# Layer 1's preparation in twenty slices, big products dealt out singly between the stages, and layer 1's first input split during layer 0's last pair

## What is computed

```python
def _layer(x, style, w, b, mw, mb, typ):
    s = style @ mw.T + mb
    weight = SCALE * w * s[:, None, :, None]
    demod = lax.rsqrt(jnp.sum(weight * weight, axis=(2, 3)) + EPS)
    weight = weight * demod[:, :, None, None]
    ...                       # conv, transposed conv + blur, conv, blur + strided conv; + b
x = x + einsum('bsd,ed->bse', cond0(x, style), identity)                 # layer 0
y = cond1(x, style)                                                      # layer 1
base = einsum('bth,oh->bto', y, W_base) + b_base
z, logits = y @ A[active], (y @ router_W + router_b)[active]
alpha = softmax(log(prior[active] + eps) + logits)
x = x + base + einsum('bteo,bte->bto', (z @ B[active]) * 2, alpha)
```

## Time and profile before

| | us |
|---|---|
| median of three runs | 1620.59 |
| lowest and highest | 1616.82, 1621.03 |
| the profiled execution | 1616.13 |
| its span, first to last instruction | 1614.3 |
| PE busy in it | 1516.0 (94%) |
| DVE, ACT, POOL busy | 1045.2, 754.4, 466.3 |

### The profile page before, as it was taken

The page is one execution under the profiler, slowest core; times in us unless marked ns, Lnnn a source line. Parts: engine busy times, 40 slices in busy tenths (PEclk is TensorE's granted clock), DMA queues, the critical chain, the costliest instruction groups (busy, mean ns, idle before and its releaser), DMA issues.

```text
span 1614.3 us, 29276 instructions
## 1 busy us (share of the span) xinstructions
PE 1516.0 (94%) x9655; PEld 1394.1 (86%) x9655; DVE 1045.2 (65%) x2447; ACT 754.4 (47%) x1675; POOL 466.3 (29%) x537
## 2 busy tenths in 40 slices
PE   4888888899999999999988999999999999999998
PEld 4677777788888888888876999999999999999998
DVE  7745676555665565566566676677667766776674
ACT  3434353254544555554443454455445545554452
POOL 2213132132233333223321322332233223322330
PEclk9999998899999999999998999999999999999999
DMA  4251321233333333333233233233323332333221
GB/s 102 79 134 54 100 58 53 58 100 104 104 104 97 85 79 102 104 104 104 78 112 113 63 104 104 78 77 104 104 78 78 104 104 79 77 104 104 80 76 65
DMA packets 54336, 145.72 MB, mean 90 GB/s; under 512 B 17233, under 2 KB 19345, under 8 KB 54306
## 3 DMA queue, kind: packets, MB, share of 16 engines
q1 hardware_dynamic: 53616, 144.96, 33.1%
q10 hardware_dynamic: 690, 0.37, 0.1%
HBM read 111.75 MB, written 33.55 MB: 90 GB/s over the span
## 4 chain that ended last, share of the span: by engine, by line
PE 81%; DVE 13%; issue 3%; DMA 1%; POOL 1%; ACT 1%; DVEq 0%; SPq 0%; ACTq 0%; POOLq 0%
PE bank L1164 25%; PE bank L1166 24%; PE bank L1165 24%; PE bank L1438 4%; DVE conv_buf L1019 2%; DVE tw L1029 2%; DVE tw L1025 1%; PE bank L1311 1%; DVE conv_buf L1022 1%; PE bank L1375 1%; DMA xraw<-x_dram 1%; DVE w_l L848 0%; PE bank L1365 0%; DVE fw_l L929 0%; DVE conv_buf L1041 0%
## 5 line engine op out<-in xcount | busy, mean ns | idle before, releaser
L1164 PE MATMUL bank<-fw_h,ct_h 128*128 128x512 f32 (+2 forms) x1280 | 462.3, 361 | 0.5 <-DVE xout L901 0.5
L1166 PE MATMUL bank<-fw_h,ct_l 128*128 128x512 f32 (+2 forms) x1280 | 454.8, 355 | 0.0
L1165 PE MATMUL bank<-fw_l,ct_h 128*128 128x512 f32 (+2 forms) x1280 | 454.2, 355 | 0.0
L376 POOL COPY conv_buf<-edge 128x4 f32 (+1 forms) x128 | 20.5, 188 | 911.3 <-DVE tw L1029 910.9
L1166 PEld LDWEIGHTS bank<-fw_h,ct_l 128*128 128x128 f32 x1280 | 242.8, 190 | 23.5
L1164 PEld LDWEIGHTS bank<-fw_h,ct_h 128*128 128x128 f32 x1280 | 243.1, 190 | 17.9 <-issue 0.8
L1165 PEld LDWEIGHTS bank<-fw_l,ct_h 128*128 128x128 f32 x1280 | 243.5, 190 | 15.5
L536 ACT ACTIVATE z_h<-bank,lam_pairs 64x256 fp32r<-64x256 f32 (+1 forms) x256 | 113.4, 443 | 214.3 <-PE bank L1166 195.1
L1006 DVE TENSOR_SCALAR z_f<-bank,lam_pairs 64x256 f32<-64x256 f32 (+1 forms) x256 | 115.2, 450 | 146.8 <-PE bank L1166 139.1
L367 POOL TENSOR_TENSOR d_l<-d_f,d_h 128x512 fp32r<-128x512 f32 x128 | 158.0, 1235 | 133.0 <-ACT d_h L522 132.9
L362 POOL TENSOR_TENSOR d_f<-xraw 128x512 f32<-128x512 f32 x128 | 169.6, 1347 | 49.8 <-DMA xraw<-x_dram 29.5
(11 more groups left out here) (219 smaller groups left out, 3108.2 us busy)
## 6 DMA issues: line engine op xcount, KB each, us to landing
xraw<-in_x_dram SPq DMA_DIRECT2D x32, 512.0 KB, 6.6
xres<-in_x_dram SPq DMA_DIRECT2D x32, 512.0 KB, 4.2
x_dram<-xout SPq DMA_DIRECT2D x32, 512.0 KB, 2.9
xraw<-x_dram SPq DMA_DIRECT2D x32, 512.0 KB, 6.2
xres<-x_dram SPq DMA_DIRECT2D x32, 512.0 KB, 4.3
out_dram<-xout SPq DMA_DIRECT2D x32, 512.0 KB, 2.9
xraw<-in_x_dram SPq DMA_DIRECT2D x32, 511.5 KB, 8.0
xraw<-x_dram SPq DMA_DIRECT2D x32, 511.5 KB, 7.6
```

Of the source, the lines that this page charges most:

```text
L1164: mm(out, wh, xh, start=start, stop=False, skip_group_check=True)
L1165: mm(out, wh, xl, start=False, stop=False, skip_group_check=True)
L1166: return mm(out, wl, xh, start=False, stop=stop, skip_group_check=True)
```

## The change

1. `PREPS` goes from 7 to 20: the same preparation is cut into twenty slices for pairs 2 to 21, and the functions on DVE, ACT and PE are cut accordingly (`prep_kernels`, `prep_roots`, `prep_tables`, `prep_pack`, `prep_selected`, `prep_base`, `prep_m13`, `prep_w1`, `prep_m4`, `prep_first_turns`, `prep_rows(k0)`). Most PE parts now stand a body ahead of the slice that reads them, behind the last big product; only two quarters of `prep_rows` stand between convolutions. Pairs 22 to 30 are the loop of ACT and DVE.
2. The big products are placed by a running number: `ffn(ly, j, lo, hi)` issues the products lo to hi - 1, and a stage can stand inside a group of three. Their order among themselves is the old one. In layer 0: 8, 11, 14, 6, 9. In layer 1: 13, 17, 20, 10, 12.
3. Layer 1's first input is loaded, and split by POOL and ACT, at the end of layer 0's last pair. On POOL it stands ahead of the three low parts of layer 1's weights (line 400). The second input's load goes ahead of the last store of layer 0.

```diff
-PREP, PREPS = 2, 7
+PREP, PREPS = 2, 20
...
+                if not n:
+                    sp.wait_ge(s["x_ready"], 2 * NPAIR)
+                    sp.wait_ge(s["stored"], stores(2))
+                    load_x(second, 0)
+                    sp.wait_ge(zs["bb_ready"], 1)
+                    for ec in range(2):
+                        load_f(second, ec)
                 sp.wait_ge(s["ffn_out"], ffn_outs(ly, NPAIR - 1))
                 store(ly, NPAIR - 2)
                 load_res(ly, NPAIR - 1)
                 if not n:
-                    sp.wait_ge(s["x_ready"], 2 * NPAIR)
-                    sp.wait_ge(s["stored"], stores(1))
-                    load_x(second, 0)
-                    sp.wait_ge(zs["bb_ready"], 1)
-                    for ec in range(2):
-                        load_f(second, ec)
+                    sp.wait_ge(second["s"]["x_ready"], 2)
+                    load_x(second, 1)
...
                     if not last:
                         x_next(j)
+                    elif not ly["lora"]:
+                        neighbours(0, layers[1])
+                        split_low(0, layers[1])
...
+                def x_next(j, h, last):
+                    act.wait_ge(s["conv_acc"], 2 * j + h + 1)
+                    if not last:
+                        x_high(ly, j + 1, h)
+                    elif not ly["lora"]:
+                        x_high(layers[1], 0, h)
...
-                x_high(0, 0, True)
-                x_high(0, 1, True)
+                if n == 0:
+                    x_high(ly, 0, 0)
+                    x_high(ly, 0, 1)
                 t_high(0)
...
                 elif i == 4:
+                    prep_scales(ly)
+                    prep_pack()
+                elif i == 5:
+                    prep_chosen(link)
+                elif i == 6:
+                    prep_roots(ly, link)
+                elif i == 7:
+                    prep_tables(ly, link)
...
                 elif i == 13:
                     prep_bias(ly, link, 1)
                     prep_b_turned(1)
+                elif i == 14:
+                    prep_bias(ly, link, 2)
                     prep_prior(link)
...
+            def ffn(ly, j, lo, hi):
+                for i in range(lo, hi):
+                    e, k = ffn_place(ly, i)
+                    part = i % 3
+                    ...
+                    last = mm(ffn_ps[e][:, 0:cols.stop - cols.start], ctf((ct_h, ct_h, ct_l)[part], k),
+                              (fw_h, fw_l, fw_h)[part][:, k, cols], ...)
...
                 def body_lora(j, composed=False):
                     if not composed:
                         stage_v(j)
-                    ffn_begin(ly, j - 1)
-                    ffn_row(ly, j - 1, 0, range(0, CHUNKS - 2))
+                    ffn(ly, j - 1, 0, 13)
                     if not composed:
                         stage_u(j)
-                    z_product(ly, j - 1)
-                    ffn_row(ly, j - 1, 1, range(0, 4))
+                    ffn(ly, j - 1, 13, 30)
                     if not composed:
                         stage_t(j)
-                    ffn_row(ly, j - 1, 1, range(4, CHUNKS - 2))
-                    ffn_row(ly, j - 1, 2, range(0, 3))
+                    ffn(ly, j - 1, 30, 50)
                     stage_conv(j, 0)
                     stage_conv(j, 1)
```

292 lines of the change are left out of this document (158 added, 134 removed).

## The result

| | us |
|---|---|
| before, median of four runs | 1620.76 (1616.82 to 1621.03) |
| after, median of four runs | 1558.97 (1556.80 to 1561.38) |
| ratio, with its 95% interval | 0.9625 (0.9604 to 0.9645) |
| the profiled execution after, and its span | 1556.8, 1555.0 |

The kernel is 61.8 us faster by the medians; the spans of the two profiled executions differ by 59.3 (1614.3 and 1555.0). The forecast was 1560.

A forecast was written before the change was run, and what follows sets the result against it. PE was taken as the busy bound, with time to win in layer 1's preparation, the passage between layers and layer 1's recurring idle. Gains 33 + 18 + 0 + 5 = 56 from 1616.1 gave 1560 us, range 1547 to 1575 (8 in 10).

The forecast's parts named there:

- Part 1: Pairs 2 to 30: cutting layer 1's preparation into twenty slices gains 33 us, bounds 22 and 42.
- The holds: PE's turns in the twenty slices: overlong DVE and ACT slices still hold them 13.7 us in all.
- The low clock: PE at 1.2 GHz behind long holds in the slices: two falls of 1.5, 3 us (bounds 0 and 10).
- the length of the slices: DVE's twenty slices, summed from 62 groups in the old profile: 0 to 4.8 us each, 44 in all.
- Part 2, layer 1: Layer 1's loop: 20 products behind T cover the convolution's wait for tw; gain 18 us, bounds 13 and 22.
- The first rival: Layer 1 keeps its length, as weight loads fill it (97%) or held time moves to T: 1578; chance 6%.
- Part 2, layer 0: Layer 0's bodies: two more products cover the convolution but V and U lose them; net 0 us, bounds ±4.
- Part 3: Passage between layers: layer 1's first input loaded and split earlier gains 5 us, bounds 1 and 8.
- the fourth rival: First input: POOL's low parts late, V(0) waits 3 us, or the chain of ends stays: 1565; chance 6%.
- third rival: PE falls to 1.2 GHz behind every one of the twenty turns: 1617 or slower; chance 1%.
- The second: Slices overrun through POOL's lock in most and 1.2 GHz behind five: 12 us more, 1572; chance 12%.
- the fifth rival: DVE's pieces shorter away from POOL, no clock fall, layer 0 gains 0.1 to 0.2 a body: 1546; chance 10%.

The follow-up runs named there:

- m2_pool_late: Changed kernel, but in layer 0's loop POOL waits for the end of conv_out(j, 1) before making the next input's low parts; 1543.08 us.
- u4_slices_only: Changed kernel with both layers' product dealings and the first input's load and split put back, leaving only the twenty slices; 1592.32 us.
- u1_l1_deal: Changed kernel with layer 1's products dealt as before (18, 18, 15, 9, 12); 1576.78 us.
- u3_x_late: Changed kernel with layer 1's first input loaded and split where it was before; 1564.50 us.

## Why the prediction was right, and where it was not

The time came out 1.0 us from the forecast. Its terms did less well than their sum, and two pieces of luck are in it. The forecast takes 56 us from the profiled execution, which was 4.5 below the median of before; by medians the kernel is 61.8 us faster, and by the spans of the profiled executions 59.3. The other is in Part 1.

**Part 1, forecast 33.** The stretch of the pairs 2 to 30 gave 33.4 in the whole change. Of the terms in it, PE's own work was put at 15 and is 17: 461.4, less twenty bodies of 21.41, less the 16.1 of holds. (Bodies without work on PE or a hold take 21.36 to 21.46, here and in `m2_pool_late`; 21.41 is the middle.) The holds were put at 13.7 and are 16.1. The low clock was put at two falls, 3 us, and the profile has none. The pairs that leave the loop were to gain 0.2 each and gain 0.3, 3.9 us for 2.6. The last two, 4.3 in its favour, pay for the first two, 4.4 against it; that is luck. Part 1 also took all seven waits of the old turn for those of slices, but the 3.98 of body 1 and the 1.10 of pair 31 are not among the seven bodies; they stayed, at 4.72 and 0.92, and this is why the page shows 21.7 and not 14 or 16.

The step that failed is the length of the slices. I read the durations of 62 groups from a stretch in which POOL ran beside part of them, and moved them as if they belonged to the operation. They belong to the place. Slices 5 and 7, put at 3.5 and 1.8, took 4.72 and 4.95, since eight of their operations now met POOL; slices 6 and 10, put at 4.8 and 4.6, took 4.30 and 5.35. The lock was named in the prediction with six delays of 0.9, worth 3 us; without it the twenty slices have 11.5 us less of holds and are 13 us shorter. The signs that were right: the longest holds are 2 to 3 us, slice 10 with 3.07 the longest, and holds follow the slice's length less 2.28, where 2.0 was taken.

**Part 1 alone** is worth 27.6 by `u4_slices_only`, and not 33. The prediction had the parts as independent, and they are not: with all three undone the mean clock of the executions falls, and POOL's lock falls on other operations. Which edit does it is open.

**Part 2, layer 1, forecast 18** (0.6 a body). Measured 0.65 a body and 17.8 by `u1_l1_deal`. The chains were read right: V's not held, U's result held to T by 0 to 0.1, and it is 0.1. The first rival (6%) is out. It was no true rival, for loads that fill 97% leave 23.8 of the 691.50 us, more than the 18 forecast. The prediction's reason against it, that overlapping loads are not a limit, is not borne out: their busy time stayed at 667 us, and the loop has come down to 672 and then to 668.

**Part 2, layer 0, forecast 0.** Measured 2.6. The working (held once becomes held twice) is what the loop shows: in a loop body U starts 0.12 late and T 0.21 late, by the distance to the product ahead of them (0.35 and 0.44 where the pace is 0.23), and the period is 21.70 for 21.63. It overlooked that thirteen more bodies are written out, whose chains on ACT and DVE are shorter: in slice 4 U starts in time and T 0.07 late.

**Part 3, forecast 5.** Measured 5.5 by `u3_x_late`; the passage is 7.2 shorter. 3.2 of it comes at the first convolution of layer 1, the rest behind it. POOL's low parts were in time, as estimated, so the fourth rival is out.

**The clock, third rival** (1%): eleven holds, five of them of 2.0 to 3.1, did not bring it down in the profiled execution. But it is a cost that comes and goes between executions, by which slices with holds of 2.4 to 2.8 take 24 us or 27. The 3 us given to it, with bounds 0 and 10, were of the right size for what other executions and kernels show.

**The second and the fifth rival.** The second (12%) named the lock in most slices, and the lock is there, but it added 2.4 us to the holds and not 12, and the clock did not fall with it. The fifth (10%) had two of its conditions, no fall of the clock in the profile and a gain in layer 0, but DVE's pieces were not shorter where they stood. With POOL moved away they are, and the time is 1543.

Left open: why the low clock comes into slice 19 in one kernel and not in another with the same hold; why the old dealing gives 21.63 in layer 0's loop now and 21.71 before the change (V to U takes 2.76 for 2.80, U to T 4.10 for 4.14); and which of the three edits brings the low clock of `u4_slices_only`.

## What to carry to other kernels

Before moving a VectorE operation, look at what GpSimd does where it was and where it will be: a duration read from a trace has the neighbour in it, and a small operation can cost as much as the whole GpSimd instruction beside it. If two helpers share a stretch, make the one with slack wait for the other; a single wait here was worth 15.9 us, nearly as much as layer 1's new dealing. And test parts of a change together as well as alone: where a clock or a lock connects them, the gains don't add.

## What was new about the chip

Most of DVE's operations of 0.16 to 0.29 us on SBUF took 1.14 to 1.25 when they started just behind the start of POOL's `d_l` (1.2) and 0.78 to 0.93 when just behind that of its `o_l` (0.85), and ended 0.02 to 0.22 behind it; started 0.02 ahead of it, one took its own 0.29. With PSUM as an input L821 took 0.22 either way. The reciprocal, 1.75, was not delayed, nor were L774 and the first L799. POOL waits for DVE as well: one `o_l` took 1.60.

A body of ACT and DVE in a loop is 0.35 us longer than the same one written out in layer 0 (21.71 and 21.35), and 0.12 in layer 1 (22.40 and 22.28), although neither engine is the bound: their chains between V, U and T are.

PE's granted clock is 1.2 GHz for a few microseconds behind some waits and not behind others of the same length: holds of 2.0 to 3.1 left it at 2.4 GHz in the changed kernel, and slices with 2.45 to 2.75 had a mean of 0.88 to 0.95 in another. The same kernel, with no part changed, took 1587.1 us at a mean clock of 0.990 and 1598.4 at 0.983.
